# A vision tower with routed experts on one core: fewer TensorE signals in each step, and one copy moved

## What is computed

```python
h = tok(x)                                   # 8x8 patches @ W + b + pos
h = h + attention(layernorm(h))              # 8 heads, softmax over keys along the
                                             # tokens and over queries along channels
z = layernorm(h)
probs = softmax(z @ gate_w + gate_b)         # 16 experts
top_probs, top_idx = top_k(probs, 2)         # two experts a token, renormed
hidden = silu(z @ w1[e]) * (z @ w2[e])       # 128 wide
h = h + sum over the two experts of top_probs * (hidden @ w3[e])
```

## Time and profile before

| | |
|---|---|
| median of the runs | 795.47 us |
| the profiled execution's own time | 794.0 us |
| its span | 792.1 us |
| TensorE matmuls | 577.0 us (73%) |
| VectorE | 443.1 us (56%) |
| ScalarE | 347.6 us (44%) |
| GpSimd | 518.1 us (65%) |
| mean granted TensorE clock | 0.86 of full |

### The profile page before, as it was taken

The page is one execution under the profiler, slowest core; times in us unless marked ns, Lnnn a source line. Parts: engine busy times, 40 slices in busy tenths (PEclk is TensorE's granted clock), DMA queues, the critical chain, the costliest instruction groups (busy, mean ns, idle before and its releaser), DMA issues.

```text
span 792.1 us, 14179 instructions
## 1 busy us (share of the span) xinstructions
PE 577.0 (73%) x3844; PEld 479.5 (61%) x3844; DVE 443.1 (56%) x1237; ACT 347.6 (44%) x753; POOL 518.1 (65%) x540
## 2 busy tenths in 40 slices
PE   5867668787899989898889988998959702973000
PEld 3455536585688668867786778686848702873000
DVE  5655653656556776776667567756755601454111
ACT  2233122152546466646564666456626701674111
POOL 2051077366771777777777777777777777777774
PEclk9987875597999999999999899989969965997555
DMA  2599032233463375528442844374344414544121
GB/s 78 111 243 388 1 96 82 71 106 94 129 186 84 78 177 146 150 54 199 135 136 55 201 128 122 75 180 115 107 117 128 113 51 123 139 101 98 40 40 30
DMA packets 168871, 93.20 MB, mean 118 GB/s; under 512 B 99680, under 2 KB 152928, under 8 KB 168800
## 3 DMA queue, kind: packets, MB, share of 16 engines
q1 hardware_dynamic: 151632, 66.71, 32.0%
q0 software_dynamic: 16384, 25.20, 11.7%
q10 hardware_dynamic: 784, 0.39, 0.2%
HBM read 45.06 MB, written 47.19 MB: 116 GB/s over the span
## 4 chain that ended last, share of the span: by engine, by line
PE 33%; POOL 26%; DVE 16%; issue 13%; DMA 6%; ACT 4%; POOLq 0%; ACTq 0%; DVEq 0%; SPq 0%
POOL sums L504 13%; POOL rows_scratch L487 9%; PE wide_ps L1013 6%; PE h_ps L1145 4%; PE y_ps L1162 3%; DMA hx<-xi_scratch 3%; DMA xi_scratch<-xi 2%; POOL hx L504 2%; POOL kexp L504 2%; PE turn_ps L1129 2%; DVE twice_y L953 2%; PE wide_ps L1105 2%; PE wide_ps L1033 2%; PE hidT_ps L1155 1%; PE wide_ps L1019 1%
## 5 line engine op out<-in xcount | busy, mean ns | idle before, releaser
L487 POOL DMA_INDIRECT rows_scratch<-z_parts,place x256 | 255.2, 997 | 128.7 <-issue 77.5
L504 POOL DMA_INDIRECT sums<-y_scratch,place x224 | 213.9, 955 | 83.6 <-issue 67.1
L1145 PE MATMUL h_ps<-w_hi,rowsT 128*128 x384 | 112.6, 323 | 39.3 <-DVE hid_all L955 34.0
L953 DVE SCALAR_TENSOR_TENSOR twice_y<-tanh,h_ps 128x256 f32<-128x256 f32 x192 | 79.6, 414 | 108.0 <-ACT tanh L601 90.1
L1145 PEld LDWEIGHTS h_ps<-w_hi,rowsT 128*128 128x128 f32 x384 | 75.5, 197 | 53.8 <-issue 52.4
L1162 PE MATMUL y_ps<-w_sb,hidT_all 128*128 x768 | 102.6, 279 | 1.0 <-ACT twice_y L614 1.0
L1145 PE MATMUL h_ps<-w_lo,rowsT 128*128 x384 | 101.5, 291 | 0.0
L1162 PEld LDWEIGHTS y_ps<-w_sb,hidT_all 128*128 128x128 f32 x768 | 99.1, 202 | 2.1 <-issue 2.1
L601 ACT ACTIVATE tanh<-h_ps 128x256 f32<-128x256 f32 x192 | 69.8, 386 | 63.7 <-PE h_ps L1145 58.5
L1129 PE MATMUL turn_ps<-ident,rows_all 128*128 128x128 f32 x384 | 62.5, 288 | 47.7 <-DMA rows_all<-rows_scratch 40.8
L955 DVE SCALAR_TENSOR_TENSOR hid_all<-twice_y,h_ps 128x256 f32<-128x256 f32 x192 | 80.7, 420 | 6.6
(11 more groups left out here) (250 smaller groups left out, 907.1 us busy)
## 6 DMA issues: line engine op xcount, KB each, us to landing
rows_all<-rows_scratch SPq DMA_DIRECT2D x96, 256.0 KB
y_scratch<-twice_y SPq DMA_DIRECT2D x96, 128.0 KB
rows_scratch<-tanh SPq DMA_DIRECT2D x3, 3072.0 KB, 19.5
xi_scratch<-xi SPq DMA_DIRECT2D x16, 256.0 KB, 3.4
rows_scratch<-z_parts,place POOLq DMA_INDIRECT x256
hx<-xi_scratch SPq DMA_DIRECT2D x14, 256.0 KB
sums<-y_scratch,place POOLq DMA_INDIRECT x224
out<-sums SPq DMA_DIRECT2D x56, 64.0 KB
```

The lines of the kernel that those rows point to most:

```text
L487: gp.indirect_dma_start(rows_dram[n], bass.IndirectOffsetOnAxis(ap=place[m % RING][:, r, j:j + 1], axis=0), z_parts[m % 2][:, j // 2, j % ...
L504: gp.indirect_dma_start(y_of[r][apart(m)][:, j // 2, j % 2, :], None, y_dram[m % 3], bass.IndirectOffsetOnAxis(ap=place[m % RING][:, r, j: ...
L953: ve.scalar_tensor_tensor(twice[:, j, :], tanh[:, j, :], 1.0, halves[:, j, 0, :], ALU.add, ALU.mult).then_inc(S["twice_done"], 1)
L1145: mm = te.matmul(h_ps[:, j * 256:(j + 1) * 256], rowsT[g % 2][:, j * P:(j + 1) * P], w[:, bass.ds(experts[g][j], 1), :, :].rearrange("d a ...
```

## The change

Signals of TensorE are merged, and ScalarE's copy of `hidT_ps` is moved.

- `rowsT_ps_ready`, `hidT_ps_ready` and `y_done` are replaced by one `step_done`, raised once a step by the last matmul of `project_out` (or of `turn`, while there is no `project_out`). Who waited for n turned groups now waits for n, who waited for n turned hidden groups for n + 3, who waited for n results for n + 4.
- `h_done` is raised by 2 at the end of a group's first projections and not by 1 after each half.
- `copy_hidT` of group g-2 stands between `turn(g+1)` and `copy_y(g-3)` in ScalarE's step, where before `copy_hidT(g-1)` stood behind `activate(g)`.
- In pairs m >= 3 the two signals for the patches (`emb_ps_ready`), the signals of quarters 0 and 1 and of 2 and 3 (`qv_ps_ready`), and the three of the attention output (`att_ps_ready`) are merged into the last one, with the same totals.

```diff
+        def rows_turned(groups):
+            return groups
+        def inner_turned(groups):
+            return groups + 3 if groups > 0 else 0
+        def projected(groups):
+            return groups + 4 if groups > 0 else 0
...
# SyncE, load_rows(g)
-                wait(sp, "rowsT_ps_ready", g - 2)
+                wait(sp, "step_done", rows_turned(g - 2))
# GpSimd, each step (and the same in scatter)
-                    wait(pool, "rowsT_ps_ready", min(s - LAG + 2, GROUPS_ALL))
+                    wait(pool, "step_done", rows_turned(min(s - LAG + 2, GROUPS_ALL)))
# ScalarE, turn(g), copy_hidT(g), copy_y(g)
-                wait(act, "rowsT_ps_ready", g + 1)
+                wait(act, "step_done", rows_turned(g + 1))
-                wait(act, "hidT_ps_ready", g + 1)
+                wait(act, "step_done", inner_turned(g + 1))
-                wait(act, "y_done", g + 1)
+                wait(act, "step_done", projected(g + 1))
# ScalarE, the loop over steps
                 if 0 <= g + 1 < GROUPS_ALL:
                     turn(g + 1)
+                if 0 <= g - 2 < GROUPS_ALL:
+                    copy_hidT(g - 2)
                 if 0 <= g - 3 < GROUPS_ALL:
                     copy_y(g - 3)
                 for m, k in steps_at(s):
                     attend(m, k)
                 if 0 <= g < GROUPS_ALL:
                     activate(g)
-                if 0 <= g - 1 < GROUPS_ALL:
-                    copy_hidT(g - 1)
# VectorE, multiply(g)
-                wait(dve, "hidT_ps_ready", g - 1)
+                wait(dve, "step_done", inner_turned(g - 1))
# TensorE
-                        te.matmul(wide_ps[:, b * 512:(b + 1) * 512], ident[:, :], pos_in[:, :, :].rearrange("p t e -> p (t e)"),
-                                  start=False, stop=True).then_inc(S["emb_ps_ready"], 1)
+                        mm = te.matmul(wide_ps[:, b * 512:(b + 1) * 512], ident[:, :], pos_in[:, :, :].rearrange("p t e -> p (t e)"),
+                                       start=False, stop=True)
+                        if m < 3:
+                            mm.then_inc(S["emb_ps_ready"], 1)
+                    if m >= 3:
+                        mm.then_inc(S["emb_ps_ready"], 2)
-                mm.then_inc(S["qv_ps_ready"], 1)
+                if m < 3:
+                    mm.then_inc(S["qv_ps_ready"], 1)
+                elif r % 2 == 1:
+                    mm.then_inc(S["qv_ps_ready"], 2)
-                        mm.then_inc(S["att_ps_ready"], 1)
+                        if m < 3:
+                            mm.then_inc(S["att_ps_ready"], 1)
+                    if m >= 3:
+                        mm.then_inc(S["att_ps_ready"], 3)
-                    mm.then_inc(S["h_done"], 1)
+                mm.then_inc(S["h_done"], 2)
                 if 0 <= g + 2 < GROUPS_ALL:
-                    turn(g + 2)
+                    mm = turn(g + 2)
                 if 0 <= g - 2 < GROUPS_ALL:
-                    project_out(g - 2)
+                    mm = project_out(g - 2)
+                if 0 <= g + 2 < GROUPS_ALL + 4:
+                    mm.then_inc(S["step_done"], 1)
```

More of the change, by code:

```diff
@@ L266, in vit_kernel @@
             past_ready owner_ps_ready owner_ready ranked place_summed place_ready
-            rowsT_ps_ready rowsT_ready h_done tanh_done twice_done hid_done hidT_ps_ready hidT_ready y_done y_ready
+            step_done rowsT_ready h_done tanh_done twice_done hid_done hidT_ready y_ready
             part_ready gated_ready result_ready""".split()
@@ L482, in scatter @@
                     if m >= 3:
-                        wait(pool, "rowsT_ps_ready", GROUPS * (m - 2))
+                        wait(pool, "step_done", rows_turned(GROUPS * (m - 2)))
                     else:
@@ L604, in copy_hidT @@
             def copy_hidT(g):
-                wait(act, "hidT_ps_ready", g + 1)
+                wait(act, "step_done", inner_turned(g + 1))
                 if g == 0:
                     act.wait_ge(S["h2_ready"], 3 * 2)
-                wait(act, "y_done", g - 1)
+                wait(act, "step_done", projected(g - 1))
                 sc.activation(hidT[g % 2][:, :], hidT_ps[:, :], ACT.Copy).then_inc(S["hidT_ready"], 1)
             def copy_y(g):
-                wait(act, "y_done", g + 1)
+                wait(act, "step_done", projected(g + 1))
                 wait_on(act, y_stored[g % 2], 16 * (g // 2))
@@ L1129, in turn @@
                     mm = te.transpose(turn_ps[:, j * P:(j + 1) * P], rows[g % 3][:, j, :, :].rearrange("p n e -> p (n e)"), ident[:, :])
-                mm.then_inc(S["rowsT_ps_ready"], 1)
+                return mm
             def project_in(g):
@@ L1155, in turn_hidden @@
                     mm = te.transpose(hidT_ps[:, j * P:(j + 1) * P], hid[g % 2][:, j, :], ident[:, :])
-                mm.then_inc(S["hidT_ps_ready"], 1)
             def project_out(g):
@@ L1163, in project_out @@
                                    w3_sb[:, bass.ds(e, 1), :].rearrange("h a d -> h (a d)"), start=True, stop=True)
-                mm.then_inc(S["y_done"], 1)
+                return mm
             setup_first()
```

## The result

After the change the kernel takes 836.18 us (median of 4 runs, 833.21 to 846.7), before 794.83 (4 runs, 793.2 to 797.77): 41.4 us more, a ratio of 1.0515 with the interval [1.0466, 1.0564]. Forecast was 812. The direction was right, the size was not.

A forecast was written before the change was run, and what follows sets the result against it. TensorE, VectorE and ScalarE bound it until GpSimd's first gather at 253.70, GpSimd afterwards. Delays of 34.9 us by step 82 less 17.8 slack gave 17.1 on 794.0, 811.1, plus 1.5 for the median: 812 us, range 799 to 821.

The forecast's parts named there:

- (f): Queries: quarter 2 starts 2.5 us later, about 3.6 us behind quarter 1's end, behind VectorE's operations, values and moved copy.
- (d): Attention output: its three parts are added only behind the last matmul, two pairs of additions more, 1.2 us.
- P: Delay that each later pair adds on TensorE, put at 8.1 us; chance of 6.3 to 9.5 us: 0.47.
- 3 P - 7.2: Delay of the end from three later pairs (4 to 6) after GpSimd's slack; 17.1 us at 8.1 us a pair.
- (g): Queries, behind quarter 3: four VectorE operations follow where the last query result came earlier, 0.8 us later.
- (h): Context: starts 2.3 us later, behind ScalarE's exponent, `turn`, the moved copy and transposes; counted as 0.9 us in later pairs.
- (j): Logits of later pairs: hidden transposes wait for the moved copy, 1.1 us; in pair 2, 0.5 us.
- second rival: TensorE's clock falls with more waiting, giving 820 to 830 us; chance of worse than 817 by any cause: 0.14.
- Behind step 83 nothing is added: Late in the kernel, TensorE's two waits for rows (40.8 us) take up its delay, and GpSimd sets the end again.
- Only the early delay: Rival: only delay before GpSimd's first gather counts, under 5.2 us a later pair; 800 to 805 us, chance 0.22.
- Faster: Rival: ScalarE's k + 0.5 pieces, freed of the copy, gain 0.5 us a step before the first gather; 789 us, chance 0.07.
- nothing moves: Rival: ScalarE reaches the copy early and only 0.8 us of later turned rows counts; 796 us, chance 0.10.

The follow-up runs named there:

- the experiment meant to isolate it: Changed kernel plus 40 small matmuls ahead of `turn_hidden` in three steps of a pair; slower chips only: 1,052.65 us against 1,004.4, then ratios 1.0526 and 1.0438 to before.

## Why the direction was right and the size wrong

Five profiles of the faster kind, in us. "Steps 53 to 65" is the stretch of the windows above; idle is its length less TensorE's busy time; "later idling" is that of GpSimd behind its first gather, beyond 0.30 us each.

| kernel | steps 53 to 65 | busy | idle | clock | first gather | later idling | own time |
|---|---|---|---|---|---|---|---|
| before | 77.9 | 68.3 | 9.6 | 1.00 | 253.7 | 0 | 794.0 |
| merged signals alone | 84.4 | 75.8 | 8.6 | 0.90 | 253.1 | 0 | 792.9 |
| after, `turn_hidden` behind k | 82.7 | 70.4 | 12.4 | 0.98 | 260.7 | 0.9 | 804.2 |
| after, pairs' signals single | 85.7 | 71.7 | 14.0 | 0.96 | 260.5 | 14.2 | 815.8 |
| after | 95.1 | 79.6 | 15.4 | 0.87 | 264.8 | 38.5 | 846.7 |

In each row the delay of the first gather plus the later idling give the time above that of before to within some 3 us.

*GpSimd sets the end, the delay ahead of its first gather counts in full.* Right. Forecast 262, measured 264.8; the mechanism (f) came out at 3.6 us for a forecast of 3.6. That 264.8 is so near owes something to luck: steps 34 to 37 made TensorE 8.2 us later for a forecast of 5.6, but the profiled execution was 2.9 us ahead of before at step 25 (the merged signals alone 2.8, the 576 extra ones 0.6).

*Signals as such are worth nothing.* Right, shown by the 576 added ones. `h_done` at no cost is not told apart from the other merged signals.

*TensorE's order turns the later copy into a wait.* Right: 62.0 us of waits where there were none, and swapping two items of TensorE's list takes back 3.2 of the 5.2 points on the faster chips and all of the loss on the slower ones.

*"A later pair: 1.1 + 0.6 + 1.0 + 3.3 + 0.9 + 1.2 (d) = 8.1 us; call it P."* This is the step that failed: it adds up waits and puts the slower matmuls behind them at nothing. The turned rows of steps 39, 52, 65, 78 and 91 stand 75.2, 77.9, 78.4 and 78.5 us apart before, and 95.7, 95.0, 92.8 and 93.0 after: P is 14 to 21 us, 16.6 on average, not 8.1. Of the 16.6 us, 8.5 are idling, nearly what the sum says, and 8.1 are longer matmuls, which it left out. With the idling alone the prediction's own 3 P - 7.2 would give 18 us and not the measured 41.4.

The steps show the same. For the second half of the queries and the context, terms (f), (g) and (h), the sum has 3.3 + 0.9 = 4.2 us. Steps 47 to 49, 60 to 62, 73 to 75 and 86 to 88 grew by 8.1 us on average: 4.6 of idling and 3.5 of longer matmuls. For the logits, term (j), it has 1.1 us. Steps 40, 53, 66 and 79 grew by 5.4, 5.6, 2.3 and 1.5 us, of which 1.0 to 1.4 are idling and the rest matmuls. Of all waits for the copy between steps 29 and 92, seven are of 3.6 or 4.6 us, and behind each of them the four transposes take 1.0 to 1.1 us in place of 0.63, the low clock. Fourteen are of 1.0 to 3.3 us, and behind two of those, in steps 40 and 53, it is the same. So in this execution the long waits come with the low clock every time, and those of about 1 us only sometimes; with the pairs' signals single it is two of the three waits of 3.8 us. With `turn_hidden` behind k no wait for the copy is longer than 1.8 us, and behind none of them are the transposes slow.

The prediction had this as its second rival, at "some 3 us" for each such stretch and two a pair, and gave it too small a chance with "the stretches added are 1 to 2.5 us long". They are up to 4.6 us long. That the clock's fall comes from the waits is read from these rows; the experiment meant to isolate it did not. These are shares of the 52.7 us of the profiled execution; how the 41.4 us divide is known only roughly. The version with the pairs' signals single shows the same pattern in its profile (815.83 us, near its median): over the four stretches 6.1 us a pair more of idling and 3.9 of longer matmuls.

*The slack.* I took it in step 83 alone, 17.8 us, and had GpSimd wait 8 to 9 us near steps 70 and 83; it waits 38.5 us, from step 41 on. In step 42 the slack is far thinner. Before, TensorE had turned the rows of step 41 at 278.14, and the first DMA of step 42 came at

```profile
281.89 0.94 POOL L504 DMA_INDIRECT sums<-y_scratch,place  x1 [0.30 <-issue]
```

so with 1.0 us from release to DMA there were 2.8 us. After, these rows are turned 17.8 us later, where my terms up to there give 7.7 + 1.2 + 1.1 + 0.6 = 10.6. The slack was used up in step 42, and every later pair then counted with all that it exceeded GpSimd's own pace, 82.6 us a pair (its first scatters at 294.36 and 376.94 before). By my own terms step 42 would not have held GpSimd up: 10.6 - 2.8 = 7.8 us is less than the 8.5 of the first gather. So it is the size of the delay that failed here, not its being read at step 83 alone. That is also why the parts do not add: the merged signals cost 0.3% alone, hidden by the slack, and those of the pairs 2.8 points (1.0233 to 1.0515) once the moved copy has used it.

*Behind step 83 nothing is added.* Nearly right: GpSimd's delay is 50.5 us at step 88, 52.0 at step 96, and stays there.

*The other rivals.* "Only the early delay" describes not the change but the version with `turn_hidden` behind k: 7.0 us late, 0.9 behind it. "Faster" and "nothing moves" fall with the late first gather. (One slip in the sum: 811.1 and 1.5 make 812.6, not 812; nothing hangs on it.)

No version beat the kernel before beyond the noise.

## What to carry to other kernels

A copy that empties the only buffer of a transpose belongs as early in its engine's list as its data allow. If it must go later, whatever stands behind the transpose on TensorE waits for it too, so move the transpose behind that work. When a wait is added to TensorE, price what follows it from rows of both clock levels: here 8.5 us of added idling a pair came with 8.1 us of longer matmuls, behind nearly all waits of 3.6 us and more, and now and then behind waits of about 1 us. And a slack hides one change only: read it at every place where the late engine is needed, the first one above all, and add up all that draws on it before calling a part free.

## What the runs showed of the hardware that was not expected

**Two kinds of chips.** The same program takes 793 to 795 us on some and 996 to 1,005 us on others, 1.26 times as long. In the traces of the slower ones the mean granted clock is 0.76 to 0.79 and not 0.85 to 0.87, and, beyond that, some of what waits for TensorE's matmuls starts late. With the merged signals alone, on such a chip:

```profile
900.92 0.28 PE L1155 MATMUL h_ps<-w_lo,rowsT 128*128 x1
...
903.57 0.66 ACT L601 ACTIVATE tanh<-h_ps 128x256 f32<-128x256 f32 x2 [3.79 <-remote]
```

The last matmul of `project_in` ends at 901.20, and tanh begins 2.4 us later. It is so only some of the time: in this trace 24 of the 64 tanh that ScalarE had idled for start more than 1 us behind a matmul's end, and the median is 0.04 us; in the profile of before on the faster kind the median is the same and none of 65 is later than 0.05 us. Later in the same place the hidden rows' transposes end at 901.64 and their copy starts at 907.14. Whether the matmuls really ended when their records say, or the signals came late, the traces do not tell; the cause stays open. What it means for a study: a change that is worth 5.2% on one kind is worth 4.5% on the other, and `turn_hidden` behind k is 1.9% slower than before on the one and even with it on the other.

**The clock falls without a new wait too.** With the merged signals alone TensorE idles no longer in steps 53 to 65 (8.6 us against 9.6), and its granted clock is 0.90 and not 1.00, worth 7.5 us of longer matmuls. Part of this can be chance: with the 576 extra signals, which change nothing else, steps 79 to 91 have a clock of 0.91 where before has 0.96, and steps 66 to 78 have 1.00 for 0.96, each worth about 2.7 us of matmuls. The Trainium skill (TensorE: Matmul & The Clock Gate, HAM oscillation — how this bites in real kernels) describes a kernel whose clock falls at each of its waits for a DMA between groups of matmuls. The waits of 3.6 and 4.6 us of the change agree (step 61: 4.57 us of waiting, then 3.16 for 1.95 us); those of about 1 us agree in steps 40 and 53 and not in steps 66, 79 and 92. For the merged signals the traces do not show which wait it was.
